# A tokenizer's finest level: patch rows turned by 96 row DMAs in place of 32 TensorE transposes

## What is computed

```
def _level(x, idx, W, b, p, gp):                 # p = 1, 2, 4; gp = 16
    t = patches(x, p)[:, idx]                    # Hilbert order
    return t.reshape(B, -1, gp * p * p * C) @ W.T + b
outs = [level0] + [interp_linear(o, 256) for o in (level1, level2)]
h = concat(outs, -1) @ Wf.T + bf                 # [16, 256, 192]
h = h + attn(layernorm(h));  h = h + fff(layernorm(h))
```

## Time and profile before

| | |
|---|---|
| time of three runs, us | median 349.04 (345.68 to 349.3) |
| the profiled execution: span from first to last instruction, us | 347.3 |
| busy share: PE, PEld, DVE, ACT, POOL | 80%, 60%, 64%, 54%, 57% |
| PE busy from 50 to 75 us | 1.86 of 25.00 us |
| PE busy from 119 to 273 us | 151.72 of 154.00 us |
| start of the first attention scores (L1307), us | 104.8 |

### The profile page before, as it was taken

The page is one execution under the profiler, slowest core; times in us unless marked ns, Lnnn a source line. Parts: engine busy times, 40 slices in busy tenths (PEclk is TensorE's granted clock), DMA queues, the critical chain, the costliest instruction groups (busy, mean ns, idle before and its releaser), DMA issues.

```text
span 347.3 us, 8076 instructions
## 1 busy us (share of the span) xinstructions
PE 279.1 (80%) x2638; PEld 209.5 (60%) x2638; DVE 222.7 (64%) x1126; ACT 189.3 (54%) x393; POOL 196.4 (57%) x419
## 2 busy tenths in 40 slices
PE   0489130037899889999999999999999999999874
PEld 0356020036697757767767776776776677886663
DVE  1014010023568786988889889889888888866882
ACT  3425000016454585686586586586577467658762
POOL 3705777600001366866776676686686686556652
PEclk9958755559999999999999999999999999999986
DMA  5601311100056083464454355355244233000028
GB/s 141 192 14 31 85 20 20 20 2 0 25 126 124 17 125 95 71 114 101 76 106 110 73 96 120 78 84 133 69 92 115 94 82 116 3 4 2 1 84 280
DMA packets 26721, 27.28 MB, mean 79 GB/s; under 512 B 6834, under 2 KB 26416, under 8 KB 26680
## 3 DMA queue, kind: packets, MB, share of 16 engines
q1 hardware_dynamic: 23176, 23.69, 29.9%
q0 software_dynamic: 1568, 2.36, 3.0%
q10 hardware_dynamic: 1936, 0.72, 0.9%
HBM read 4.34 MB, written 3.15 MB: 22 GB/s over the span
## 4 chain that ended last, share of the span: by engine, by line
PE 67%; another core or an unknown queue 12%; DVE 6%; DMA 4%; ACT 3%; issue 3%; SPq 2%; POOL 1%; POOLq 0%; DVEq 0%; ACTq 0%
PE bank L1311 7%; PE bank L1345 7%; PE bank L1367 7%; PE bank L1249 4%; PE bank L1268 4%; PE bank L1307 3%; PE bank L1349 3%; PE bank L1285 3%; PE bank L1287 3%; PE bank L1257 3%; PE bank L1370 3%; PE bank L1228 2%; PE bank L1240 2%; SPq L296 2%
## 5 line engine op out<-in xcount | busy, mean ns | idle before, releaser
L857 DVE CUSTOM_DVE_ANT_0 C<-bank,MASKV 128x256 bf16<-128x256 f32 (+1 forms) x384 | 112.4, 350 | 17.9 <-PE bank L1311 14.0
L572 ACT ACTIVATE PT<-bank 128x512 f32<-128x512 f32 x144 | 80.0, 606 | 45.0 <-PE bank L1345 43.5
L372 POOL TENSOR_SCALAR_AFFINE_SELECT PT<-PT 128x256 f32<-128x256 f32 x144 | 66.3, 473 | 0.0
L350 POOL TENSOR_TENSOR PART<-RES,PART 128x256 bf16<-128x256 f32 (+1 forms) x31 | 27.9, 902 | 34.3 <-ACT PART L566 34.3
L368 POOL TENSOR_TENSOR CARRY<-CARRY 1x1 f32<-1x1 f32 x96 | 17.6, 183 | 46.4 <-ACT PT L572 46.4
L345 POOL DMA_INDIRECT G<-x,I x32 | 30.2, 944 | 21.0 <-PE bank L1157 11.6
L1228 PE MATMUL bank<-RH,LH 128*128 128x192 f32 x64 | 13.8, 359 | 26.0 <-ACT LH L509 24.2
L857 DVE DVE_READ_ACCUMULATOR2_ANT MX<- 128x1 f32 x384 | 31.9, 83 | 0.1
L805 DVE TENSOR_TENSOR RH<-bank,BFB 64x384 f32<-64x384 f32 x8 | 4.5, 560 | 41.5 <-remote 32.0
L1367 PE MATMUL bank<-PT,VA 128*32 128x256 f32 x384 | 30.7, 390 | 0.1
L1311 PE MATMUL bank<-KS,QS 96*128 96x256 bf16 x144 | 27.9, 275 | 1.0 <-DVE MX L857 0.8
(11 more groups left out here) (167 smaller groups left out, 648.7 us busy)
## 6 DMA issues: line engine op xcount, KB each, us to landing
QS<-PART SPq DMA_DIRECT2D x72, 96.0 KB, 3.6
KS<-PART SPq DMA_DIRECT2D x72, 96.0 KB, 3.4
out<-HT SPq DMA_DIRECT2D x7, 384.0 KB, 3.4
KSL<-PART SPq DMA_DIRECT2D x24, 96.0 KB, 3.3
QSL<-PART SPq DMA_DIRECT2D x24, 96.0 KB, 3.6
G<-x,I POOLq DMA_INDIRECT x42
out<-HT SPq DMA_DIRECT2D x2, 192.0 KB, 3.4
WFS<-wft ACTq DMA_DIRECT2D x2, 144.0 KB
```

Of the source, the lines that this page charges most:

```text
L350: pool.tensor_tensor(parts(b)[2][:, ROUNDS[w], :], RES[:, ROUNDS[w], :], parts(b)[1][:, ROUNDS[w], :], ALU.subtract).then_inc(p2_ok, 1)
L372: pool.affine_select(out=e, in_=e, compare_op=ALU.is_ge, fill=0.0, base=0, pattern=[[0, n], [1, P]], channel_multiplier=-1).then_inc(cut_o ...
L572: nc.scalar.activation(PT[:, v, :], BANK[T_BANK[(SU * par + v) % 2]][:, :], ACT.Exp, scale=SCALE).then_inc(exp_ok, 1)
L857: ins = nc.vector.tensor_tensor_reduce(JUNK[:, n:n + keys], bank[:, j * keys:(j + 1) * keys], MASKV[:, S - keys:S], 1.0, LOWEST, ALU.add, ...
```

## The change

The eight `patches_t` and the ACT copies behind them go. Instead each of the 48 pixel rows of each t is turned by a DMA of its own: `G0[:, t, k, :]`, 16 numbers (64 bytes) on each of 128 partitions, to `LH[k, t, :, :]`, 8 KB on one partition. That makes 96 DMAs; SP issues the even rows, ACT the odd ones, each after the gather that brings the row (one semaphore a gather). `LH` is laid out [row, t, token, image], so that a token product reads its 128 weight columns 16 numbers apart. `sums` takes two images in a product (four instead of eight), and DVE's additions read either half of the bank. `ORDER` and the hand-written orders of PE, ACT and DVE change with it.

```diff
-            LH = tok("LH", [P, NT, P])
+            LH = tok("LH", [P, TT, P, B])
...
-        ORDER = ((0, 0), (0, 1), (0, 2), (0, 3), (1, 0), (0, 4), (0, 5), (0, 6), (0, 7)) + tuple((1, q) for q in range(1, PAIRS))
+        ORDER = ((0, 0), (0, 1), (0, 2), (1, 0), (1, 1), (0, 3), (1, 2), (0, 4), (0, 5), (0, 6), (0, 7)) + tuple((1, q) for q in range(3, PAIRS))
...
+            def turned(t, g):
+                sp.wait_ge(g0_in[t][g], 16)
+                for k in range(F0 * g, F0 * (g + 1)):
+                    if k % 2 == 0:
+                        sp.dma_start(LH[k:k + 1, t, :, :], G0[:, t, k, :]).then_inc(lh_in[t], 16)
+            sp.wait_ge(lhb_ok, TT)
+            for t in range(TT):
+                for g in range(GP):
+                    turned(t, g)
...
-            patches_t(0, 0)
-            patches_t(0, 1)
-            tokens(0, 0)
-            tokens(0, 1)
...
+            act.wait_ge(lhb_ok, TT)
+            for g in range(GP):
+                turned(0, g)
+            for g in range(GP):
+                turned(1, g)
+                if g in (7, 10, 13):
+                    tokens(0, (7, 10, 13).index(g))
+            tokens(1, 0)
+            deviations(1, HEADS)
+            tokens(1, 1)
+            front(first)
+            tokens(0, 3)
...
-            def sums(q):
-                if q >= 4:
-                    pe.wait_ge(dve_d, q + 1)
-                else:
-                    pe.wait_ge(act_a, 9 + q // 4)
...
+            def sums(i):
+                pe.wait_ge(act_a, 9 + i // 2)
                 for j in range(2):
-                    b = 2 * q + j
-                    ins = nc.tensor.matmul(BANK[4 + q % 4][T1:P, j * D:(j + 1) * D], E1[:, b * T1:(b + 1) * T1], WFS[:, 1, :], start=True, stop=True)
+                    q = 2 * i + j
+                    ins = nc.tensor.matmul(BANK[4 + i][:, j * D:(j + 1) * D], E1[:, q * P:(q + 1) * P], WFS[:, 1, :], start=True, stop=True)
                 ins.then_inc(pe_d, 1)
...
-                pe.wait_ge(dve_d, 5 + q)
-                pe.wait_ge(lh_ok, 4 * t + q // 2 + 1)
+                pe.wait_ge(dve_d, 4 + 2 * (q // 2 + 1))
+                pe.wait_ge(lh_in[t], 16 * GP * F0)
...
-                    ins = nc.tensor.matmul(BANK[2 + n % 2][:, j * D:(j + 1) * D], LH[:, TT * b + t, :], RH[:, b, :], start=True, stop=True)
+                    ins = nc.tensor.matmul(BANK[2 + n % 2][:, j * D:(j + 1) * D], LH[:, t, :, b], RH[:, b, :], start=True, stop=True)
```

More of the change, by code:

```diff
@@ L182, in vit_tower_kernel @@
         g2_in = sem("g2_in")
-        pt_ps, lh_ok, lhb_ok, rhc_ok = sem("pt_ps"), sem("lh_ok"), sem("lhb_ok"), sem("rhc_ok")
+        lhb_ok, rhc_ok = sem("lhb_ok"), sem("rhc_ok")
         ld_w6, ld_late, carry_init = sem("ld_w6"), sem("ld_late"), sem("carry_init")
         g1_in = sem("g1_in")
-        g0_in = [sem(f"g0_in{t}") for t in range(TT)]
+        g0_in = [[sem(f"g0_in{t}_{g}") for g in range(GP)] for t in range(TT)]
+        lh_in = [sem(f"lh_in{t}") for t in range(TT)]
         pe_a, pe_d = sem("pe_a"), sem("pe_d")
@@ L518, in _, with turned @@
                 nc.scalar.activation(E1[:, c * 512:(c + 1) * 512], BANK[2 + c][:, :], ACT.Identity, bias=BC[:, 1:2]).then_inc(act_a, 1)
+            def turned(t, g):
+                act.wait_ge(g0_in[t][g], 16)
+                for k in range(F0 * g, F0 * (g + 1)):
+                    if k % 2:
+                        act.dma_start(LH[k:k + 1, t, :, :], G0[:, t, k, :]).then_inc(lh_in[t], 16)
             def tokens(t, q):
@@ L685, in _ @@
             values(first)
-            tokens(0, 7)
-            tokens(1, 1)
-            patches_t(1, 3)
-            tokens(1, 2)
-            front(second)
-            deviations(2, SECOND)
-            tokens(1, 3)
-            tokens(1, 4)
+            tokens(1, 2)
+            tokens(0, 4)
+            tokens(0, 5)
+            front(second)
+            tokens(0, 6)
+            tokens(0, 7)
             first_part(second, 0)
@@ L698, in _ @@
             values(second)
+            tokens(1, 3)
+            tokens(1, 4)
             first_step()
@@ L800, in _ @@
                                       BANK[4 + q][0:HALF, :].rearrange("p (b g t) -> p g b t", b=4, g=2)).then_inc(dve_d, 1)
-            def sums(q):
-                dve.wait_ge(pe_d, 5 + q)
-                nc.vector.tensor_tensor(RH[T1:P, 2 * q:2 * q + 2, :], BANK[4 + q % 4][T1:P, 0:2 * D].rearrange("p (b d) -> p b d", b=2),
-                                        BFB[T1:P, :].rearrange("p (a d) -> p a d", a=1).broadcast_to([T1, 2, D]), ALU.add).then_inc(dve_d, 1)
+            def sums(i):
+                dve.wait_ge(pe_d, 5 + i)
+                rows = RH[T1:P, 4 * i:4 * i + 4, :].rearrange("p (j b) d -> p b j d", j=2)
+                for h in range(2):
+                    own = slice(T1 * h, T1 * (h + 1))
+                    nc.vector.tensor_tensor(rows[:, h, :, :], BANK[4 + i][own, 0:2 * D].rearrange("p (j d) -> p j d", j=2),
+                                            BFB[own, :].rearrange("p (a d) -> p a d", a=1).broadcast_to([T1, 2, D]), ALU.add).then_inc(dve_d, 1)
             done = [0]
@@ L993, in first_low @@
                 nc.vector.tensor_tensor(PART[2][:, ROUNDS[1], :], RES[:, ROUNDS[1], :], PART[1][:, ROUNDS[1], :], ALU.subtract).then_inc(p2_ok, 1)
-            for q in range(PAIRS):
-                sums(q)
+            for i in range(B // 4):
+                sums(i)
             statistics(0, 0)
             statistics(0, 1)
+            statistics(0, 2)
             statistics(1, 0)
@@ L1536, in _ @@
             first, second = Image(0, 0), Image(0, 1)
-            for q in range(PAIRS):
-                sums(q)
-            patches_t(0, 0)
-            patches_t(0, 1)
+            for i in range(B // 4):
+                sums(i)
             tokens(0, 0)
             tokens(0, 1)
-            patches_t(0, 2)
-            patches_t(0, 3)
             tokens(0, 2)
-            tokens(0, 3)
-            patches_t(1, 0)
             tokens(1, 0)
-            tokens(0, 4)
-            patches_t(1, 1)
-            tokens(0, 5)
-            tokens(0, 6)
+            tokens(1, 1)
             xn_t(first)
@@ L1556, in _ @@
             nc.tensor.matmul(BANK[O_BANK[0]][:, 0:D], BVC[:, 1:2].broadcast_to([P, P]), WP[:, 1, :], start=False, stop=True).then_inc(bpv_ps, 1)
+            tokens(0, 3)
             pe.wait_ge(ld_const, 16 * N_CONST)
-            patches_t(1, 2)
             heads(first)
-            tokens(0, 7)
-            tokens(1, 1)
-            patches_t(1, 3)
             tokens(1, 2)
+            tokens(0, 4)
+            tokens(0, 5)
             pe.wait_ge(bpv_ok, 1)
             xn_t(second)
+            tokens(0, 6)
+            tokens(0, 7)
+            heads(second)
             tokens(1, 3)
             tokens(1, 4)
-            heads(second)
             pe.wait_ge(ld_ones, 16 * RING)
-            pe.wait_ge(lh_ok, 8)
             first_step()
```

56 lines of the change are left out of this document (13 added, 43 removed).

## The result

The changed kernel took 368.84 us (median of 4 executions, 365.22 to 373.7) against 348.62 for the kernel before on the same chip: 1.068 times as long by the ratio on record, 95% interval 1.061 to 1.075; the quotient of the medians is 1.058. Its profiled execution has a span of 372.0 us, 24.7 more than that of before. It is the slowest of the four; the medians differ by 20.2. (A ratio compares undisturbed executions only, so it is not always the quotient of the medians.)

The account below looks back on a forecast made before the run. It took the opening's 42.59 us wait, ending at 74.6, as the bound. Terms -5.3 + 0.7 + 0.8 - 0.4 = -4.2 us off the 349.04 median gave 344.8 us, range 340 to 353.

Parts of the forecast that it names:

- Added, 96 row DMAs at 0.63: SP and ACT issue each row in 0.63 us; SP starts at 39.31, starts its last at 68.9, level with the gathers.
- T0: Start of the token product of t = 1, pair 0, that image 0 waits for: 82.30 before, forecast 77.0.
- rival D: Rows of 64-byte pieces land slower than issued; break-even 0.83 us a row, 357.2 us at 1.0; chance 0.14.
- Landing 2.08: A row DMA lands 2.08 us after its issue, taken from the smallest fold of many partitions into two.
- ACT's waits between its issues: Three token copies between ACT's row issues wait for PE's counts, taken 6.33 us apart; T0 at 77.0.
- Low clock, 0.7: Product of t = 1 runs at PE's low clock, +0.7 us; 3.4 more if it stayed low through the heads, not taken.
- Strided weights: Weights read 16 numbers apart cost 0.16 us a load, 0.65 a product, two products on the path; 0.8 us taken.
- Sums and stacks at nothing: Half as many `sums`, all before 34 us, and SP's first stack 5 us earlier: no effect on the time.
- The rule weighed: Skill page advises against small DMAs; one behind the other 96 rows would take 192 us, by row spacing 30 a queue.
- E: Late counts belong only to the profiled execution, so nothing is to be won: about 349 us; chance 0.16.
- C: ACT's wait replaces the old one, counts 10.55 us apart, T0 = 82.1: 349.9 us; chance 0.20.
- B: ACT sees PE's counts at once, nothing holds it, T0 = 72.6: 340.4 us; chance 0.18.

Follow-up runs that it names:

- the pair with and without idle gathers: Changed kernel with patch rows filled by two plain transfers: 368.63 us with the 32 gathers writing a spare tile, 350.05 us without gathers.
- the comparison above: Changed kernel reading neighbouring columns (366.93 us): first scores 24.13 us behind T0, against 28.75 in the changed kernel and 25.67 in full-clock kernels with strided reads.
- the gathers that nobody reads: Kernel before with patch rows filled by two plain transfers and its 32 gathers writing an unread tile: 347.84 us; without gathers 309.61 us.
- the two real kernels: Kernel before and changed kernel, each with a POOL fill of 384 columns behind each gather: 349.34 us and 364.39 us.
- the kernel with early gathers: Kernel before without POOL's wait for PE's eighth count, so the finest level's gathers start at once after the second level's: 348.65 us, ratio 1.0076.
- the paced rows: Changed kernel with a POOL fill of 384 columns behind each gather, gathers 1.55 us apart: 364.39 us.

## Why the prediction was wrong, step by step

*What bounds the kernel: right in place, not in cause.* The 42.59 us were the bound and stand in all executions; they belong to the gathers' density, which the change leaves as it was. I had written that no row names the cause, and went on as if SyncE and ACT could not be held by it too. The row was there: the delay covered all that ran beside the gathers, and I priced the row DMAs from moves that end at 33.94, when the gathers had run for 5 us.

*Added, 96 row DMAs at 0.63: the step that failed.* The price is right where no dense gathers run (0.64). Beside them it is 1.43 to 1.71 on SyncE, by the pair with and without idle gathers through the gathers alone. SyncE's start was 44.77, not 39.31 (its four loads of ones ahead took from 38.55 to 42.32; without gathers it is 40.15), and its last issue 92.79, not 68.9. That is T0: 92.79 + 2.29, where I had 77.0. The mean over its 48 rows is 48.02 / 47 = 1.02 us, past the break-even of 0.83 that rival D named. A slip of my own beside it: by its own numbers SyncE could not have t = 0 landed by 52.7, but 39.31 + 23 x 0.63 + 2.08 = 55.9.

*Landing 2.08: right.* 2.29 in the chain.

*ACT's waits between its issues: right as a risk, not what decided.* It waited from 68.79 to 79.87 for the first product; that product waited for SyncE's rows, not for a late count. Only DVE's last additions were late (8.84 us).

*Low clock, 0.7: I had the larger price and took the smaller.* The granted clock was 0.5, the lower of its two levels, from 39.7 to 104.5, so the product of T0 (2.90 for two against 1.54), `xn_t` (1.11 against 0.66) and the first of the heads (1.53 against 1.03) all ran at it. For a clock that stays low through the heads I had named 3.4 us more and not taken them; by the comparison above it cost some 3.1. Next to that, 1.6 us are left between T0 and the first scores with the loads packed and the clock full by `xn_t`, where I had 0.7 - 0.4.

*Strided weights: a load nearly right, a product too dear, the count too small.* At the full clock a load takes 316 ns against 190, 0.13 more, where I had 0.16; at the low clock there is no difference (medians 332 in the strided kernel, 337 before), so T0's product pays nothing. Two products take 2.09 us against 1.57 at the full clock, 0.26 more each, not 0.65, since loads run beside the products. But eight stand between T0 and the first scores, not two, and I had put all the later ones into "the 13 us in which PE and ACT wait for SP's 12 stack DMAs". PE hardly waits there: it was busy 10.87 and 14.35 us of these two stretches,

```profile
95.00:108.00 13.00, 10.87 (x43) 9.55 (x44) 4.91 (x23) 2.73 (x8) 0.00 (x0) 0.63 0.01 2
108.00:124.00 16.00, 14.35 (x72) 13.23 (x72) 7.76 (x23) 8.03 (x19) 2.49 (x3) 0.89 0.52 92
```

and at the end of the token products it runs ten filler products (L1288, x20 with two passes each) whatever has landed. In before, that filler ended at 104.7, just when the last stack landed (101.11 + 3.60): the wait I saw in the chain had no slack in it. So what the products ahead of the filler cost is on the path: the eight would make 2.1 us, the comparison above leaves some 1.5, and I had 0.8. In the time of the kernel before the layout alone costs more, 5.4 us by the ratio (2.5 to 8.3).

*Sums and stacks at nothing: right.* 1.0006 for the sums; the 12th stack is issued 20.6 us after T0 (115.76 - 95.21), before 18.8.

*The rule weighed.* The Trainium skill's page "DMA: Bandwidth & Descriptors", section "Rules for kernel authors", spoke against the change, and the change lost; but not by the sum that I had set for it. Without gathers 96 rows of 64-byte pieces cost 32 us on two queues and land in 2.5 us, far from the estimate of 192 (the page fits its 2.0 us to DMAs issued by GpSimd; these were not). In kind the rule is borne out: without gathers the kernel with transposes took 309.61 us and this one 350.05. The same page's section "SWDGE vs HWDGE vs iDMA" says that VectorE can lock GpSimd out of the memory in which it writes its DMA descriptors, and that DMAs issued from SyncE and ScalarE never touch that path and are immune to that interference. It speaks of VectorE's interference, which no run here tests. The gathers' own is another: by gathers alone the same 48 issues of SyncE take 49.67 us instead of 31.97.

*The rivals.* D had the outcome in kind (T0 89.4, 357.2 at c = 1.0) with the wrong mechanism: the issue was slow, not the pieces, and its sum lacked SyncE's late start and the 6.2 us behind T0. E is refuted by the gathers that nobody reads. C's and B's question, how late ACT sees its counts, did not come up. D's chance of 0.14 was too low: I held the SyncE rows with a median of 0.594 against it, and all of them start after 93 us, where no gather runs.

*What adds up.* T0 +12.9 and the way to the first scores +6.2 make 19.1 of the profile's 24.7. The other 5.6 lie behind the first scores, 248.0 us of this execution against 242.5. All profiles of kernels with row DMAs have 244.5 to 248.0 us there, all with transposes and packed weights 242.0 to 243.3; what makes the difference no run shows.

*T0 as the measure: not enough.* I had written that the change is worth what it moves the end of the opening. Without gathers T0 is at 74.50, 7.8 us ahead of the kernel before and 2.5 ahead of my 77.0, and yet the time is 350.05 us, ratio 1.005 (0.996 to 1.015). So rows at 0.64 throughout would not have given the 4.2 us either: behind T0 the change costs more than the 1.1 us that I gave it.

## What to carry to other kernels

Take the price of an operation from rows of the stretch in which it will run; a queue that is free at another time may share something with what runs there now. An unowned delay that ends soon after a neighbour ends may be the neighbour's: test that first, by taking it out, letting nobody read it, or spacing it, before work is taken off the engines that suffer. A milestone that comes earlier is not yet time saved: look at what stands behind it, and at which clock it ran in each profile, before a difference of two profiles is given to a cause. And a wait in the chain that ends just when the waiting engine is done with its own work has no room for more work.

## What the hardware showed that I had not expected

- Indirect gathers on POOL 1.25 us apart delay others: PE's counts by 6 to 10 us each, a row on SyncE from 0.64 to 1.43 us and more, until 7 to 10 us after the last one's issue (67.52 to 74.6 in before, 68.10 to 78.1 in the changed kernel). At 1.55 apart both are gone in the two real kernels; at 1.44, started earlier, counts are still taken 9 to 14 us after PE is done. An estimate that each gather keeps something busy for about 1.43 us, the pace of SyncE's rows, fits two kernels (28.8 + 32 x 1.43 = 74.6, when all is free in before; 5.2 + 42 x 1.43 = 65.2 in the kernel with early gathers, whose 42 gathers start at 5.17 and whose late count comes at 65.04) and is 3 us short in the changed one. What is shared no run shows.
- Two queues that move neighbouring rows of 64-byte pieces at the same moment: landing 27 us after the issue, at 12 GB/s; on rows 24 apart the DMA engines are busy a sixth as much and move 21.
- Landings can be late too: 7.82 us for a gather at the end of the paced rows.
- At the full clock weights 16 numbers apart load in 316 ns for 128 columns, packed ones in 190; at the low clock in 332 and 337 (medians).
